# A fused attention and experts kernel: order of the self-attention turns, splits of weights and inputs, handover to the experts, end

## The reference

```python
x = x + cross_attention(layernorm(x), ctx, ctx, mask)   # 16 heads of 32, biases
x = x + self_attention(layernorm(x))                    # q and k are RMS-normed per head, softmax over 32 keys
x = x + ffn(layernorm(x))
# ffn: xm = k0*x[s-1] + k1*x[s] + k2*x[s+1]; choice = argmax(tanh(xm@Wo1+bo1)@Wo2+bo2) of 9 experts
#      y = (xm@W1[e]+b1[e])@W2[e]+b2[e] of the chosen e; out = layernorm(x+y)*gamma+beta
```

## Time and profile before

| what | value |
|---|---|
| median of three runs | 794.41 us |
| the profiled execution, own time | 793.65 us |
| its span, first to last instruction | 791.7 us |
| granted TensorE clock, mean | 0.990 |
| VectorE, ScalarE, POOL busy | 49%, 42%, 24% |
| load of 1024 KB into `raw`, issue to landing | 4.8 us |
| store of 256 KB, issue to landing | 2.1 us |

### The profile page before, as it was taken

One profiled execution on the slowest core, in us unless ns is written; L12 is line 12 of the kernel. 1 busy time (PEld: TensorE's weight loads), 2 busy tenths in 40 slices (PEclk: granted clock), 3 DMA queues, 4 the chain that ended last, 5 costly groups with the idle time before them and its releaser, 6 DMA issues. The chain is left out here.

```text
span 791.7 us, 20456 instructions
## 1 busy us (share of the span) xinstructions
PE 751.6 (95%) x8258; PEld 587.8 (74%) x8258; DVE 390.5 (49%) x942; ACT 335.9 (42%) x690; POOL 187.7 (24%) x245
## 2 busy tenths in 40 slices
PE   5999999999999999999999999799999989999994
PEld 4777778778877877787788777677877766677673
DVE  5544434343443344243424546756667675633546
ACT  4435444443444344444435455224554545521210
POOL 0001000010010010010100202555777770692002
PEclk9999999999999999999999999999999999999998
DMA  9211110011011101101120114120000022100011
GB/s 331 71 48 55 54 55 23 33 53 53 0 53 53 53 0 53 53 1 52 53 49 4 53 53 108 66 84 3 0 0 4 2 69 80 41 1 0 1 54 53
DMA packets 9471, 37.05 MB, mean 47 GB/s; under 512 B 2633, under 2 KB 2889, under 8 KB 6482
## 3 DMA queue, kind: packets, MB, share of 16 engines
q1 hardware_dynamic: 9426, 36.42, 13.6%
HBM read 34.32 MB, written 2.10 MB: 46 GB/s over the span
## 5 line engine op out<-in xcount | busy, mean ns | idle before, releaser
L94 PE MATMUL pj<-W_hi 128*128 128x512 f32 x512 | 209.1, 408 | 9.7 <-DVE W_lo L594 9.7
L96 PE MATMUL pj<-W_lo,W_hi 128*128 128x512 f32 x512 | 201.2, 393 | 0.0
L95 PE MATMUL pj<-W_hi,W_lo 128*128 128x512 f32 x512 | 200.4, 391 | 0.0
L94 PEld LDWEIGHTS pj<-W_hi 128*128 128x128 f32 x512 | 96.8, 189 | 40.7 <-issue 22.4
L96 PEld LDWEIGHTS pj<-W_lo,W_hi 128*128 128x128 f32 x512 | 96.7, 189 | 21.4
L95 PEld LDWEIGHTS pj<-W_hi,W_lo 128*128 128x128 f32 x512 | 97.0, 189 | 17.9
L235 POOL COPY q_b<-Q_T 128x128 f32 (+1 forms) x32 | 9.3, 291 | 415.8 <-PE tp L358 348.9
L492 ACT ACTIVATE K<-pj,bk 128x512 f32<-128x512 f32 x64 | 44.1, 690 | 136.1 <-PE pj L96 136.1
L654 DVE CUSTOM_DVE_ANT_0 m_flat<-sc,mask 128x257 f32<-128x257 f32 x64 | 25.3, 425 | 115.4 <-PE tp L358 94.1
L507 ACT ACTIVATE p_flat<-m_flat,nmax 128x257 f32<-128x257 f32 x128 | 63.8, 501 | 24.5 <-DVE nmax L654 24.5
L499 ACT ACTIVATE V<-pj 128x512 f32<-128x512 f32 x64 | 38.2, 598 | 73.7 <-PE pj L96 71.8
(11 more groups left out here) (287 smaller groups left out, 1329.3 us busy)
## 6 DMA issues: line engine op xcount, KB each, us to landing
raw<-ctx_dram SPq DMA_DIRECT2D x15, 1024.0 KB, 4.8
raw<-w_dram SPq DMA_DIRECT2D x6, 768.0 KB, 4.9
raw<-w_dram SPq DMA_DIRECT2D x4, 1024.0 KB, 4.8
x_nat<-x_dram SPq DMA_DIRECT2D x2, 1024.0 KB, 11.7
out_dram<-raw SPq DMA_DIRECT2D x8, 256.0 KB, 2.1
raw<-wk_dram SPq DMA_DIRECT2D x2, 512.0 KB, 5.4
p_flat<-ctx_dram SPq DMA_DIRECT2D x2, 512.0 KB, 6.8
m_flat<-wv_dram SPq DMA_DIRECT2D x1, 1024.0 KB, 9.9
```

Source lines behind the costliest of these rows:

```text
L94: eng.matmul(out, a_hi, b_hi, start=first, stop=False)
L95: eng.matmul(out, a_lo, b_hi, start=False, stop=False)
L96: return eng.matmul(out, a_hi, b_lo, start=False, stop=last)
```

## The change

- Semaphores `pe_seen`, `dve_seen`, `pool_seen` are made once for both blocks and take the place of `s_seen`, `s_ready`, `o_seen`; the increment of `x0_made` goes.
- Turn 1: `weight_split(4)` and `Wp_lo` are made earlier in the turn. Turn 2: `head_norm` of tile 0 comes first on VectorE; `wo_proj(4)` has its own bank.
- Turns 6 to 8: PE starts with `qkv` 0, then `out_proj`, then `qk_transposes`. In all turns from 2, `z2_transposes` goes ahead of `weighted_sum`, and z2's parts ahead of o2's.
- `xm_hi` and `xm_lo` of the first half are made tile by tile in turns 4 to 8, `xm_lo` on VectorE; `g_hi`, `g_lo` in turns 6 and 7.
- Behind the gate `spread(0)`, `spread_evac(0)`, `out_proj(10)`, `w_split(2)`, `hidden_rows` and `take_x2(10)` change places.
- End: POOL makes each of the four roots by `pow`; tiles 4 and 6 are normalised by ScalarE, scaled by POOL, and the addition is POOL's for 4 and VectorE's for 6.
- VectorE's loop over turns 3 to 5 is written out.

The diff, without the semaphores' hunks and cut to the lines that change with a neighbour:

```diff
@@ -897,6 +898,7 @@
     stats_made, centred = sem("stats_made"), sem("centred")
+    root_step, shift4_made, normed, fin0 = sem("root_step"), sem("shift4_made"), sem("normed"), sem("fin0")
     ex_in, exw_in, ln_in, stored = sem("ex_in"), sem("exw_in"), sem("ln_in"), sem("stored")
@@ -917,8 +919,8 @@
-        if isinstance(t, int) and t <= LEAD + 1:
-            return (pw[0][:, :], pw[1][:, :], pa[:, 0, :], pa[:, 1, :])[t]
+        if isinstance(t, int) and t <= LEAD + 2:
+            return (pw[0][:, :], pw[1][:, :], pa[:, 0, :], pa[:, 1, :], pa[:, 2, :])[t]
         return pw[0][:, :]
@@ -960,8 +962,13 @@
                 eng.dma_start(beta, row_on_all(io["beta"])).then_inc(ln_in, 16)
-        for i, t in enumerate((0, 1, 2, 3, 6, 7, 4, 5)):
-            eng.wait_ge(fin, i + 1)
+        for t in range(NH):
+            eng.wait_ge(fin, t + 1)
+            eng.dma_start(out[t], y(t)).then_inc(stored, 16)
+        eng.wait_ge(fin0, 1)
+        eng.dma_start(out[NH], y(NH)).then_inc(stored, 16)
+        for i, t in enumerate((5, 7, 6)):
+            eng.wait_ge(fin, NH + i + 1)
             eng.dma_start(out[t], y(t)).then_inc(stored, 16)
@@ -1062,11 +1069,7 @@
         mix(NT - 4)
-        eng.wait_ge(xmhi, 1)
-        eng.tensor_tensor(xm_lo[:, :, :], O_T[:, :, 0:HT], xm_hi[:, :, :].bitcast(F32), ALU.subtract).then_inc(xmlo, 1)
         head_norm(0, NT - 1)
-        eng.wait_ge(g_split, 1)
-        eng.tensor_tensor(g_lo[:, :, :], g_raw, g_hi[:, :, :].bitcast(F32), ALU.subtract).then_inc(g_split, 1)
         head_norm(1, NT - 1)
@@ -1082,12 +1085,30 @@
             eng.tensor_tensor(x_nat[:, t, :], x_nat[:, t, :], beta, ALU.add).then_inc(xb_made, 1)
-        for t in range(2):
-            y_t = y(NH + t)
+        def y_root(t):
+            one = slice(t, t + 1)
             eng.wait_ge(stats_made, NH + t + 1)
-            eng.tensor_scalar(y_t, y_t, mv4[:, t, 0:1], None, ALU.subtract).then_inc(centred, 1)
-            eng.wait_ge(centred, 2 * t + 1)
-            eng.tensor_tensor(y_t, y_t, gamma, ALU.mult).then_inc(centred, 1)
+            eng.tensor_scalar(tmp4[:, one], mv4[:, t, 1:2], LN_EPS, 1.0, ALU.add, ALU.mult).then_inc(root_step, 1)
+            eng.wait_ge(root_step, 2 * t + 1)
+            eng.tensor_tensor(rstd4[:, one], tmp4[:, one], power[:, one], ALU.pow).then_inc(root_step, 1)
+            eng.wait_ge(root_step, 2 * t + 2)
+            if t in (0, 2):
+                eng.tensor_scalar(shift4[:, one], mv4[:, t, 0:1], rstd4[:, one], -1.0,
+                                  ALU.mult, ALU.mult).then_inc(shift4_made, 1)
+        def y_scale(t):
+            eng.wait_ge(normed, t // 2 + 1)
+            eng.tensor_tensor(y(NH + t), y(NH + t), gamma, ALU.mult).then_inc(centred, 1)
+        eng.wait_ge(fin, NH)
+        y_root(0)
+        y_scale(0)
+        y_root(1)
+        eng.wait_ge(centred, 1)
+        eng.tensor_tensor(y(NH), y(NH), x_nat[:, NH, :], ALU.add).then_inc(fin0, 1)
+        y_root(2)
+        y_root(3)
+        y_scale(2)
@@ -1114,7 +1135,7 @@
                 eng.wait_ge(olo_made, t - 1)
-            if has(t, LEAD + 2):
+            if has(t, LEAD + 3):
                 eng.wait_ge(qk_out, 2 * (t - LEAD - 1))
@@ -1148,6 +1169,8 @@
                     eng.wait_ge(x1_made, 1)
+                elif isinstance(it, int) and it == 2:
+                    eng.wait_ge(qk_out, 2)
                 elif has(it, -LEAD):
@@ -1169,6 +1192,8 @@
             need(eng, o2lo_made, u)
+            if isinstance(it, int) and it == 2:
+                eng.wait_ge(x1_made, LEAD + 3)
             eng.sem_inc(pe_seen, 1)
@@ -1211,9 +1236,13 @@
                 wo_proj(it + LEAD)
-            if has(it, 3):
+                if has(it, 3):
+                    out_proj(it)
+            if not has(it, -LEAD):
+                qkv(it, 0)
                 out_proj(it)
-            if isinstance(it, int) and it == 2:
+                qk_transposes(it)
+            elif isinstance(it, int) and it == 2:
                 qkv(it, 0)
@@ -1226,17 +1255,17 @@
                 qkv(it, 2)
+            if not isinstance(it, int) or it >= 2:
+                z2_transposes(it)
             if has(it, 2):
                 weighted_sum(it)
-            if not isinstance(it, int) or it >= 2:
-                z2_transposes(it)
             if has(it, 3):
             eng.wait_ge(g_split, 2)
-            eng.wait_ge(xmlo, hf + 1)
+            eng.wait_ge(xmlo, NH + hf)
             if hf == 0:
@@ -1312,9 +1341,9 @@
+        qkv(NT, 0)
         out_proj(NT)
         qk_transposes(NT)
-        qkv(NT, 0)
         scores(NT)
@@ -1329,12 +1358,12 @@
         hidden(1)
+        spread(0)
         weighted_sum(NT + 1)
-        spread(0)
         spread(1)
-        out_proj(NT + 2)
         hidden(2)
         spread(2)
+        out_proj(NT + 2)
         z3_transposes(NT + 1)
@@ -1435,6 +1464,8 @@
                 weight_split(2)
+            if isinstance(it, int) and it == 1:
+                weight_split(4)
             if has(it, 2):
@@ -1448,13 +1479,11 @@
                 square(it, 1)
-            if has(it, 2):
-                o2_split(it)
-            if isinstance(it, int) and it == 1:
-                weight_split(4)
             eng.wait_ge(z2T_done, it + 1)
             eng.activation(z2_hi[:, :, :].rearrange("p c t -> p (c t)"), pt[0][:, :], ACT.Copy).then_inc(z2hi_made, 1)
+            if has(it, 2):
+                o2_split(it)
             if has(it, 3):
@@ -1464,11 +1493,19 @@
-        def xm_split(hf):
-            eng.wait_ge(mix_made, NH * (hf + 1) + 1)
-            if hf:
-                eng.wait_ge(h_done, E)
-            eng.activation(xm_hi[:, :, :], O_T[:, :, hf * HT:(hf + 1) * HT], ACT.Copy).then_inc(xmhi, 1)
+        def xm_split_tile(u):
+            cols = slice(u * P, (u + 1) * P)
+            eng.wait_ge(mix_made, u + 2)
+            eng.activation(xm_hi[:, :, cols], O_T[:, :, cols], ACT.Copy).then_inc(xmhi, 1)
+        def xm_split_rest():
+            eng.wait_ge(mix_made, NT + 1)
+            eng.wait_ge(h_done, E)
+            eng.activation(xm_hi[:, :, :], O_T[:, :, HT:T], ACT.Copy).then_inc(xmhi, 1)
+        def g_hi_split():
+            eng.wait_ge(ex_in, 6 * 16)
+            eng.activation(g_hi[:, :, :], g_raw, ACT.Copy).then_inc(g_split, 1)
@@ -1495,13 +1532,14 @@
             body(it)
+            if it >= NH:
+                xm_split_tile(it - NH)
+            if it == NT - 2:
+                g_hi_split()
         qk_evac(NT)
         z3_make(NT)
-        xm_split(0)
         square(NT, 0)
         exps(NT)
-        eng.wait_ge(ex_in, 6 * 16)
-        eng.activation(g_hi[:, :, :], g_raw, ACT.Copy).then_inc(g_split, 1)
         square(NT, 1)
@@ -1513,19 +1551,19 @@
         w_split(1)
-        w_split(2)
+        spread_evac(0)
         o2_split(NT + 1)
-        z3_make(NT + 1)
-        spread_evac(0)
         hidden_split(0)
         spread_evac(1)
+        z3_make(NT + 1)
         hidden_split(1)
+        w_split(2)
+        spread_evac(2)
+        hidden_split(2)
         eng.wait_ge(proj_done, NT)
         z3_make(NT + 2)
-        spread_evac(2)
         mix_parts(NT + 1)
-        hidden_split(2)
         w_split(3)
@@ -1537,12 +1575,16 @@
             hidden_split(k)
-        xm_split(1)
+        xm_split_rest()
         tanh(1)
             hidden_split(k)
+        for t in (0, 2):
+            eng.wait_ge(shift4_made, t // 2 + 1)
+            eng.activation(y(NH + t), y(NH + t), ACT.Identity, bias=shift4[:, t:t + 1],
+                           scale=rstd4[:, t:t + 1]).then_inc(normed, 1)
@@ -1656,16 +1698,23 @@
             else:
+                if isinstance(it, int) and it == 2:
+                    head_norm(it - 2, 0)
                 if has(it, -LEAD):
                     take_x1(it + LEAD)
+                if isinstance(it, int) and it == 2:
+                    head_norm(it - 2, 1)
                 x1_stats(it, ch)
-            if has(it, 2):
+            if has(it, 3):
                 head_norm(it - 2, 1)
-            if has(it, 3):
                 take_x2(it)
                 q_evac(it)
+            if isinstance(it, int) and it == 1:
+                eng.wait_ge(whi, 5)
+                eng.tensor_tensor(w_lo[4], raw[:, 0, :].rearrange("p (c n) -> p c n", c=CT), w_hi[4].bitcast(F32),
+                                  ALU.subtract).then_inc(wp_lo, 1)
             if has(it, 2):
@@ -1676,17 +1725,16 @@
                 v_evac(it)
-                head_norm(it - 1, 0)
             elif has(it, 1):
                 v_evac(it)
-            if has(it, 2):
-                o2_split(it)
             eng.wait_ge(z2hi_made, it + 1)
                               z2_hi[:, :, :].rearrange("p c t -> p (c t)").bitcast(F32), ALU.subtract).then_inc(z2lo_made, 1)
+            if has(it, 2):
+                o2_split(it)
             if isinstance(it, int) and it == 0:
@@ -1694,10 +1742,6 @@
```

(49 more changed lines are left out.)

27 lines of the change are left out of this document (14 added, 13 removed).

## The result

The changed kernel takes **800.57 us** (median of 4 runs, 799.57 to 800.88) where the kernel before takes 794.4. The ratio is **1.0077**, with a 95% interval of 1.0059 to 1.0094: slower by some 6.2 us. The forecast was 797.9, slower by 3.5. The profiled execution took 800.43 us, with a span of 798.9 (before: 793.65 and 791.7).

A forecast was written before the change was run, and what follows sets the result against it. TensorE was taken to bound the kernel, busy 751.6 of 791.7 us. Terms: -3.4 + 5.3 - 2.1 + 0 - 0.4 + 4.1 = +3.5 us, giving 797.9 (forecast's chance 0.55); range 791.2 to 800.6.

The forecast's parts named there:

- the string on GpSimd: Turns 6 and 7: later residual, then GpSimd's fixed queue, makes each turn 20.0 us; +5.3 us together.
- Rival B: Turns 6 and 7: GpSimd's string does not set the turn, take_x2 to z2's remainder under 11 us; 789.8 us, chance 0.15.
- The swap gives 0: Turns' ends: z2's remainder takes o2's slot in the same queue, and PE then asks for z2's; 0 us.
- Turn 8 to `out_proj(9)`: Turn 8 through the gate: gate at 18.45, `out_proj(9)` at 21.3 after the turn's start instead of 23.44; -2.1 us.
- Start: Second and third turn: 4.34 us wait removed, scores(2) at 516.2 instead of 519.63; -3.4 us, ends -4.8 and -1.9.
- Handover: `out_proj(9)` to z3 transposes: new 3.1 us wait on take_x2 replaces a 1.7 us wait and slow clock; 0 us.
- End: After PE's last matmul: VectorE work removed, POOL and ScalarE work added, port conflicts; -0.2, store another -0.2 us.
- Rival C: Second turn and end: POOL and VectorE do not hold each other, and the clock holds; 790.8 us, chance 0.10.
- Clock: PE's four new waits (3.1, 3.1, 2.1, 3.1 us): three bring a clock fall at 1.4 each; +4.1 us, ends 0 and +6.
- Rivals A and C: A, whole kernel: clock holds at 2.4 GHz (793.8 us) or falls once (795.2), chance 0.20; C has its own line.

The follow-up runs named there:

- a3: Changed kernel with GpSimd's head_norm(0) of turns 6, 7 and the tail put ahead of with_bproj and mix, TensorE's new order kept: 796.77 us, ratio 1.0042.
- b2: Changed kernel with GpSimd's with_bproj and mix ahead of norm3 in turns 6, 7 and the tail, TensorE's new order kept: 791.89 us, ratio 0.9984.
- a1: Changed kernel with TensorE's old order in turns 6, 7 and 8 (output projection, transposes, query projection) put back: 791.94 us, ratio 0.9966.
- b1: a1 with the old order of the remainders as well (o2 ahead of z2, weighted sum ahead of the z2 transposes): 788.71 us, ratio 0.9928.
- c3: b1 with the gate's inputs split in one piece in the tail, remainders of the half and gate weights back on GpSimd: 793.67 us, ratio 0.9981.
- b3: Changed kernel with one more wait: VectorE's Wp_lo split in the second turn begins only after GpSimd's norm1 shift: 802.56 us, ratio 1.0102.
- c2: b1 with the second and third turn as before the change (Wp_lo split at the second turn's end, old projection bank): 790.66 us, ratio 0.9942.
- a2: Changed kernel with extra, overwritten matmuls keeping TensorE busy in the waits ahead of turns 7, 8 and the first gate: 798.08 us, ratio 1.0044.
- a4: Changed kernel with the old handover behind the first gate (TensorE, VectorE and ScalarE orders as they were): 797.86 us, ratio 1.0038.
- c1: b1 with the last tile's take_x2 earlier, as in b4: 785.77 us, ratio 0.988.
- b4: Changed kernel with VectorE's take_x2 of the last tile ahead of the third hidden layer's remainder: 799.94 us, ratio 1.0056.

## Why the prediction was right, and where its sizes were off

**Turns 6 and 7, the string on GpSimd: right.** The forecast's chain (take_x2 later by one projection, then norm3, bproj, mix and the power, multiply, k's squares, v, z2's remainder) is what the trace shows link by link: take_x2 at 588.97, the power from 597.27, the multiply at 600.33, z_lo at 602.13, start at 602.87. 19.84 us was forecast as 20.0, the wait of 3.1 came as 2.94 and 3.04. a3 moved one link and won 1.0 us a turn, b2 took two links out and won 2.0, a1 and b1 took the cause out. Rival B (the string does not set the turn) is shown wrong: it wanted under 11 us from take_x2 to z2's remainder, and these are 13.16 apart.

**"The swap gives 0": right only beside the new order of PE.** There the first work of a turn asks for z2's remainder, and the swap puts it first. Beside the old order, which asks for o2's, it costs 0.6 us a turn and falls (a1 against b1: 38.67 to 34.65). The two parts of the change belong together, and each was costed with the other in place only.

**Turn 8 to `out_proj(9)`: right, with the falls outside it.** Link by link: the residual comes 7.32 us after the turn's start (5.94 in turn 6, which has no fall), the power ends 10.04 behind it (forecast 9.7), the last `xm_lo` tile ends at 644.34 and the gate starts at 644.44, and the gate's 12 matmuls take 4.38 us (2.88 in b1, at full clock). Without the 1.4 and the 1.5 of the two falls, the 24.47 us are 21.6, where the forecast had 21.3.

```profile
631.67 0.69 DVE L1623 TENSOR_TENSOR x_nat<-pw,x_nat 128x512 f32<-128x512 f32 x1 [4.23 <-PE pw L97]
```
```profile
638.40 3.31 POOL L1019 TENSOR_TENSOR rms<-ms_eps,power 128x16 f32<-128x16 f32 x1 [0.21 <-POOL ms_eps L1015]
```

What the forecast did not separate: the tile splits alone bring 4.4 us (c3), and the string takes a part back. With the string two links shorter and no fall the stretch is 20.73 us (b2), with the old order of PE 19.18 (a1).

**Start: -2.6 where -3.4 was taken.** The step that was off is the power, which was let begin just ahead of the split (502.11 against 502.13) and so run free. It began 0.07 us behind it and was held: 2.63 us in place of 0.55, shift 2.05 us late in place of 1.4. The forecast's bounds were -4.8 and -1.9. That the split can't simply be put elsewhere is b3's. c2 shows that what the start wins stays won. The Trainium skill (SBUF — State Buffer, "Who interferes with whom") says that a VectorE instruction with two SBUF inputs contends with a GpSimd instruction that reads SBUF, that the lock on the shared ports is exclusive, and that the order of issue decides who is blocked. a3 (1.64 for 0.69), the changed kernel (2.63 for 0.55) and b3 (3.36 and 3.35) agree; the power of 128x16 in the earlier trace rows, inside which the old split began and still took 2.28, does not.

**Handover: 0 forecast, a loss measured.** The wait on take_x2 was forecast as 3.1 us and is 2.56 (take_x2 ends at 671.77, the transposes start at 671.88), and the stretch is 0.4 shorter. But the forecast stopped at the z3 transposes. Behind them the kernel loses 3.6 us: some 1.6 for the fall that follows the wait, 0.5 at the second gate (1.06 in place of 0.56 of waiting), 1.4 for the fall at 735 (the same stretch takes 115.64 to 115.65 us in a1, a2, a3, b2 and c2, which have the wait and its fall but not the one at 735). In the medians a4 and c1 agree with 2.7 and 2.9 us. The wait at the second gate hangs on the new handover: it is 1.06 to 1.28 us in every trace that has it, and 0.40 in the three in which it is undone or its wait shortened (a4, b4, c1); by which path, 45 us later, was not tried. The fall at 735 does not hang on it: c1 has it with the short wait, and those five lack it with the long one.

**End: -0.95 where -0.4 was taken.** VectorE's last two instructions run at 0.75 and 0.69: the port conflicts with GpSimd that the forecast counted did not come (Rival C had that right for the end, and wrong for the start, where the power was held). The store at the end is as long as before (2.7 us from DVE's last instruction).

**Clock: 5 falls where 3 were taken.** All four new waits brought one, at 1.4 to 1.6 each, and a fifth (1.4) came at a wait of 0.78 us that is also in the kernel before. This term (+4.1 forecast, some +7.5 measured) is the largest of the misses, and takes the time from 797.9 to the range's upper end: 800.57 lies inside 800.6 by 0.03 us, and that it does is luck: the other misses (start +0.8, end -0.55 and smaller ones) nearly cancel, and the median is 0.14 us above the profiled execution, where the forecast added 0.76. Rivals A and C needed a clock that holds: wrong here. The count compares two executions and not two kernels: of the 54 executions of the kernel before that were timed beside the experiments, 46 have a mean clock of 0.981 to 0.986, near the changed kernel's 0.984, and only 7 the 0.990 of its profiled one. The median of the 46 is only 0.5 us above that of the 7, so the further falls cost it little; no trace shows where they are.

## What to carry to other kernels

When a piece of work is moved ahead on the bounding engine, follow what it delays through every queue to the next start of the loop: here 3 us of delay met a GpSimd queue with fixed order. Putting that queue's idle-time work ahead of its wait took back 8.7 us with the move kept (b2); undoing the move and the swap took back 11.9 (b1), so the move itself was not worth keeping here. Cost each part of a change both with and without the others; the new order and the swapped remainders fit only each other, and the fastest version has neither. And where TensorE gets new waits of two to three microseconds, count a fall of the clock for most of them: the waits of 2.56 to 2.58 us ahead of the z3 transposes brought one in eight traces of ten, those of 0.97 to 1.42 us at the turns' starts in none.

## What was not expected of the hardware

**The length of a wait does not decide whether the clock falls.** The same 2.0 us wait brought it down twice and left it once within one execution (a1). 2.94 us ahead of turn 7 did in the changed kernel (0.59), and 2.92 us did not in a4 (1.00). 2.57 us ahead of the z3 transposes did in a1 and did not in b1. 0.82 us at scores(2) did in b3 and b4 and not in the changed kernel. The waits of 1.41 and 1.42 us at the turns' starts never did, in the kernel before, in b1 and in c1. Executions of one kernel so differ by whole falls, as the two groups of c3 suggest, and b2's times run from 789.0 to 798.3. A single profile can be 4 us off its kernel's median (a4), and medians can hide a gain that the trace shows (b4). What decides whether a wait brings a fall is open.

**A start that is earlier by a tenth of a microsecond can hold the other engine for its whole length**: the split, begun 0.07 us ahead of the power, cost it 2.1 us, and the addition, 0.17 us ahead of the multiply, cost that 0.95. That the other order would have been free was not tried for these two pairs.
